# Block inversion on 16x16 instead of 32x32 blocks, a bias product over 128 rows, and a new order of all engines' lists

## The reference, cut to what matters

```python
def step(S, inp):                      # attention, token by token
    q_t, k_t, v_t, beta_t, alpha_t = inp
    S = S * alpha_t[..., None, None]
    kv = jnp.einsum('bhk,bhkv->bhv', k_t, S)
    S = S + jnp.einsum('bhk,bhv->bhkv', k_t, (v_t - kv) * beta_t[..., None])
    o_t = jnp.einsum('bhk,bhkv->bhv', q_t, S)
    return (S, o_t)
...
logits = flat_x @ W_router + b_router  # experts: the best 2 of 8
for e in range(NUM_EXPERTS):
    h = jax.nn.relu(flat_x @ W1[e] + b1[e])
    y = h @ W2[e] + b2[e]
    final_output = final_output + y * w[:, None]
```

## Time and profile before

| what | value |
|---|---|
| median of three runs | 1421.86 us |
| profiled execution: span | 1397.9 us |
| outside the span, runs less span | 21.2 to 25.0 us |
| PE, DVE busy in the span | 1199.9, 1164.4 us |
| ACT, POOL busy in the span | 832.0, 707.9 us |
| setup and first round | 0 to 133.8 us |
| 15 steady rounds | 133.8 to 1145.4 us, 67.44 us each |
| last round, routing's tail | 1145.4 to 1232 us |
| experts | 1232 to about 1371 us |

### The profile page before, as it was taken

How to read it: one execution, slowest core, us unless ns; L and a number is a source line. 1 busy time by engine, 2 the same in 40 slices (tenths; PEclk the granted TensorE clock), 3 DMA queues, 4 the chain that set the end, 5 groups by cost and what they waited for, 6 DMA issues and landing times.

```text
span 1397.9 us, 34191 instructions
## 1 busy us (share of the span) xinstructions
PE 1199.9 (86%) x12203; PEld 944.0 (68%) x12203; DVE 1164.4 (83%) x2531; ACT 832.0 (60%) x2536; POOL 707.9 (51%) x598
## 2 busy tenths in 40 slices
PE   0355999999999999999999999999999989479991
PEld 0233868686868687777777777777777767358881
DVE  6878898989898998989898989897989783578875
ACT  1252666666666666657566666756566655358884
POOL 3151727464555656473828292928192822235552
PEclk9997999999999999999999999999999998789996
DMA  6031212222221222131313141313121223432225
GB/s 208 0 98 32 73 35 73 47 69 62 54 63 53 62 54 64 52 68 48 84 34 91 28 98 25 103 28 88 30 85 43 73 55 98 104 96 78 76 65 181
DMA packets 163176, 97.10 MB, mean 69 GB/s; under 512 B 115623, under 2 KB 148269, under 8 KB 161988
## 3 DMA queue, kind: packets, MB, share of 16 engines
q1 hardware_dynamic: 124932, 82.25, 21.6%
q10 hardware_dynamic: 33536, 4.20, 2.1%
q0 software_dynamic: 4544, 8.47, 1.9%
HBM read 73.31 MB, written 24.61 MB: 70 GB/s over the span
## 4 chain that ended last, share of the span: by engine, by line
DVE 37%; PE 21%; POOL 17%; issue 10%; DMA 9%; SPq 3%; ACT 3%; POOLq 0%; DVEq 0%; ACTq 0%
DVE blkT L1060 9%; POOL kq L637 9%; DVE Y_sb L1056 9%; DMA blkN<-scr_n 4%; PE kx L1553 3%; POOL decay L629 3%; POOL rows_in L609 2%; DVE Gs L1204 2%; POOL kq L620 2%; DMA scr_n<-area 2%; PE rc L1717 2%; SPq L477 2%; DVE blkN L1047 1%; DVE area L1170 1%; DVE Y_sb L1043 1%
## 5 line engine op out<-in xcount | busy, mean ns | idle before, releaser
L637 POOL TENSOR_TENSOR kq<-tapA,area 128x256 f32<-128x256 f32 x256 | 252.0, 998 | 93.6 <-DVE area L1146 92.8
L758 ACT ACTIVATE area<-pj,taps 128x256 f32<-128x256 f32 x256 | 123.1, 481 | 142.7 <-PE pj L1567 136.5
L1056 DVE TENSOR_TENSOR Y_sb<-blkT,blkN 128x4 f32<-128x4 f32 (+18 forms) x304 | 169.5, 558 | 10.5
L609 POOL DMA_INDIRECT rows_in<-rowbuf,dest x64 | 64.6, 1009 | 202.1 <-DVE dest L1132 175.2
L1143 DVE SCALAR_TENSOR_TENSOR tapA<-pj,taps,tapA 128x256 f32<-128x256 f32 x256 | 122.2, 477 | 53.4 <-ACT tapA L758 51.6
L1553 PE MATMUL kx<-kq 128*128 128x128 f32 x1024 | 141.0, 285 | 20.0 <-ACT area L767 9.6
L1553 PEld LDWEIGHTS kx<-kq 128*128 128x128 f32 x1024 | 128.7, 197 | 38.4 <-issue 21.8
L620 POOL TENSOR_TENSOR kq<-kq,area 128x1024 f32<-128x1024 f32 x64 | 151.1, 2362 | 0.0
L1060 DVE TENSOR_REDUCE blkT<-Y_sb 128x2 f32<-128x4 f32 (+18 forms) x304 | 142.4, 469 | 5.2
L758 ACT ACTIVATE tapA<-pj,taps 128x256 f32<-128x256 f32 x256 | 123.0, 480 | 0.0
L1146 DVE SCALAR_TENSOR_TENSOR area<-pj,taps,area 128x256 f32<-128x256 f32 x256 | 121.4, 474 | 0.0
(11 more groups left out here) (307 smaller groups left out, 3613.2 us busy)
## 6 DMA issues: line engine op xcount, KB each, us to landing
area<-scr_alpha SPq DMA_DIRECT2D x32, 512.0 KB, 4.2
area<-scr_acum SPq DMA_DIRECT2D x32, 512.0 KB, 4.0
blkN<-scr_n SPq DMA_DIRECT2D x32, 256.0 KB, 4.4
area<-rows_in SPq DMA_DIRECT2D x39, 130.0 KB, 2.3
scr_n<-area SPq DMA_DIRECT2D x128, 32.0 KB, 1.6
area<-rows_out SPq DMA_DIRECT2D x4, 1024.0 KB, 8.1
rows_in<-rows_in SPq DMA_DIRECT2D x8, 260.0 KB, 3.8
kq<-in_x SPq DMA_DIRECT2D x4, 512.0 KB, 6.2
```

Of the source, the lines that this page charges most:

```text
L637: nc.gpsimd.tensor_tensor(dst[:, n % H, :], tapA[:, n % RING, :], tapB[:, n % RING, :], ALU.add).then_inc(conv_done, 1)
L758: ins = nc.scalar.activation(dst[:, n % RING, :], pj[n % 2][:, k:k + GT], ACT.Copy, scale=taps[:, t, k:k + 1])
L1056: ins = nc.vector.tensor_tensor(p4, bc(blkT[:, r0:, j:].rearrange("p r (o m) -> p r o m", o=1), [128, nr, w, wd]), bc(blkN[:, j:j + w, j:] ...
```

## The change

- **Blocks of 16.** The diagonal's 16x16 blocks, 128 of them, lie one in a partition. `bi` reads two quarters of every 32x32 block, rows of 64 bytes. `invert` has 8 pairs of product and sum (2, 18, 50, 98, 162, 242, 338 and 450 elements), three short operations of 128 and 16 elements, a memset, and a copy that writes the transpose, blkR. `rdiag` is gone.
- **From 16 to 32.** The inverses go out to scr_r and scr_a and come back into R's diagonal and TA. New steps: `y16` on PE (64 matmuls of 32x16, four 32-row bands in turn), `ye` on ACT (eviction of 128x256), `r16` on PE (64 of 16x16), `re` on DVE (four of 16x16x16), `td.0` and `td.1` on DVE (two transposes and one of 32x512).
- **New waits.** `nm` waits for the merge's y64_mm, `at` for o_mm, `kd` for sd_mm, `zt` for g_ready, `diag` for scale_ready, `ti` and `tj` for u_mm.
- **Bias.** b2_both has 128 rows, 126 of them zero, and L1713's matmul takes all 128.
- **Setup.** par_eye and its DMA go, scr_r is zeroed by one DMA.
- **Order.** ORDER is rewritten; the stand-ins stay 7 and 8.

```diff
-        SOLVE = [(j, 2) for j in range(BLK - 2, PAIR0 - 2, -2)] + [(j + i, 1) for j in range(PAIR0 - 2, -2, -2) for i in range(2)]
-        INV = 5 + 2 * len(SOLVE)
+        SOLVE = list(range(SUB - 2, -2, -2))
+        INV = 6 + 2 * len(SOLVE)
...
                         for side in range(2):
-                            sp.dma_start(blkN[64 * side:64 * side + 64, :, :], scr_n).then_inc(blk_in, 16)
+                            half_ = slice(SUB * side, SUB * side + SUB)
+                            sp.dma_start(blkN[64 * side:64 * side + 64, :, :], scr_n[:, half_, half_]).then_inc(blk_in, 16)
...
-                        sp.dma_start(scr_t.rearrange("q (a p) m -> p q a m", p=2)[0], blkT[0:64, :, :]).then_inc(t_out, 16)
+                        sp.dma_start(scr_r[:, 0:SUB, 0:SUB], blkR[0:64, :, :]).then_inc(t_out, 16)
+                        sp.dma_start(scr_a, blkT[0:64, :, :]).then_inc(t_out, 16)
...
+                        if g is not None:
+                            sp.wait_ge(u_mm, halves(g, GC - 1, U - 1))
+                        for b in range(NB):
+                            sp.dma_start(TA[BLK * b:BLK * b + SUB, :, :], a_blocks[b]).then_inc(t_in, 16)
...
+                elif s == INV - 1:
+                    ins = nc.vector.tensor_copy(blkR[:, :, :], blkT.rearrange("p r j -> p j r"))
                 else:
...
+                    j = SOLVE[(s - 5) // 2]
+                    n = SUB - 1 - j
+                    p4 = prod[:, 0:n * 2 * n].rearrange("p (r k m) -> p r k m", k=2, m=n)
...
                     elif step == "nm":
                         c, u = arg
                         dve.wait_ge(kk_ready, a * HALVES + U * c + u + 1)
+                        if g is not None:
+                            dve.wait_ge(y64_mm[c], rounds(g))
...
+            def small_blocks(g, a, r, step):
+
+                bank_free((step,), g, a, r)
+                n = GC * H * SUB
+                if step == "y16":
+                    pe.wait_ge(t_in, g * (32 * NB) + 32 * NB)
+                    y = ob[1][:, 0:n].rearrange("p (q j) -> p q j", j=SUB)
+                    for q in range(GC * H):
+                        for b in range(NB):
+                            r_ = slice(BLK * b, BLK * b + BLK)
+                            ins = mm(y[r_, q], Nm[r_, q // H, q % H, r_], TA[r_, q, :], start=True, stop=True)
...
-                    mm(o, ones[0:2, :], b2_both[:, ds(e, 1), :].rearrange("p o n -> p (o n)"), start=True, stop=False)
+                    mm(o, ones[:, :], b2_both[:, ds(e, 1), :].rearrange("p o n -> p (o n)"), start=True, stop=False)
```

Of the new ORDER the line that brings `st.0.1` behind the inversion's first steps:

```diff
+            first.13 taps.11 u.0.1 first.14 xl.1 taps.12 sd.0.0 inv.0 ue.0.1 last.6 kk.1.1 inv.1 proj.11 sm v.1.0
+            inv.2 taps.13 last.7 proj.12 st.0.1 taps.14 ktr.0.0 no.1 kd.0.0 inv.3 ks.1.0 last.8 sq.0.0 inv.4 proj.13
```

More of the change, by code:

```diff
@@ L264, in preln_delta_moe_kernel @@
-            st.1.1 xs.1 tj sc
+            proj.0 taps.0 first.0 last.0 y16 ye first.1 proj.1 al.0 taps.1 re r16 ka.0 taps.2 td.0 proj.2 taps.3
+            proj.3 first.2 v.0.0 me.1.0 first.3 aq.0 m.1.0 me.0.0 first.4 ac.0 ks.0.0 taps.4 first.5 proj.4 last.1
+            me.1.1 td.1 m.0.0 taps.5 m.1.1 scan.0 sp.0 taps.6 proj.5 first.6 v.0.1 me.0.1 al.1 first.7 proj.6 me.1.2
+            last.2 first.8 m.0.1 scale.0 proj.7 nm.0.0 rhs.0.0 m.1.2 diag.0 first.9 taps.7 ks.0.1 nm.0.1 no.0 m.0.2
+            me.0.2 scan.1 last.3 m.1.3 taps.8 st.0.0 proj.8 me.1.3 kk.0.0 nm.1.0 me.0.3 last.4 m.0.3 nm.1.1 rhs.0.1
@@ L303, in bank_of @@
                 return ("ob", "kx")[i], j % 2
+            if step in ("y16", "r16"):
+                return "ob", 1
             return None
@@ L317, in released @@
                 return ((x2_ready, chunks(b, i)),)
+            if step in ("y16", "r16"):
+                return (({"y16": y16_sb, "r16": r16_done}[step], rounds(b)),)
             if step == "m":
@@ L571, in _ @@
             nc.gpsimd.memset(T64[:, :, :, :], 0.0)
+            nc.gpsimd.memset(TA[:, :, :], 0.0)
             nc.gpsimd.memset(R, 0.0)
@@ L1245, in _ @@
             over_t = lambda t: bc(t.rearrange("p (t o) -> p t o", o=1), wide)
+            dve.wait_ge(sd_mm, NG * HALVES)
+            chain(nc.vector.memset(b2_both, 0.0), t_step, steps)
             dve.wait_ge(f_b2, 32)
             chain(nc.vector.tensor_scalar(b2_hi, b2_raw, WSCALE, None, ALU.mult), t_step, steps)
-            chain(nc.vector.scalar_tensor_tensor(out=b2_both, in0=b2_raw, scalar=WSCALE, in1=b2_hi, op0=ALU.mult,
+            chain(nc.vector.scalar_tensor_tensor(out=b2_both[0:2], in0=b2_raw, scalar=WSCALE, in1=b2_hi, op0=ALU.mult,
                                                  op1=ALU.subtract), t_step, steps)
@@ L1590, in finish @@
                 def finish(step, arg):
-                    if step == "m":
+                    if step in ("y16", "r16"):
+                        small_blocks(g, a, r, step)
+                    elif step == "m":
                         if arg != [1, 3]:
```

182 lines of the change are left out of this document (106 added, 76 removed).

## The result

The changed kernel takes **1534.07 us** (median of 4 runs, 1529.23 to 1535.36), the kernel before beside it 1422.34: ratio **1.078 [1.075, 1.080]**. Forecast were 1397.8, range 1364 to 1434. It is 7.8% slower, and it lies outside the range.

The account below looks back on a forecast made before the run. PE was taken to bound the steady rounds and experts, the inversion only the first round. First round -10, last round +2.4, steady rounds -4.5, experts -12: -24.1 us, 1421.9 to 1397.8 us, range 1364 to 1434.

Parts of the forecast that it names:

- The small products: y16 and r16 on PE: 1.2 us each, bounds 1.0 and 4.0, so PE's work rises 2.4 us a round.
- the forecast's 67.5: Steady round: 22.3 + 43.2 + 0.8 + 1.2 = 67.5 us against 67.8, -4.5 us over 15 rounds.
- POOL's lateness at `kk.0.1`: Head of the round: POOL's longer list puts kk.0.1 at 22.3 us instead of 20.2, 2.1 us later.
- No overlap of small products: Rival for y16 and r16: 4.0 us each instead of 1.2, +5.6 a round, 1470 us; chance 0.05.
- the grown wait: Rival at v.1.1: PE's wait for the scratch trip reaches 3.4 us, other pauses return, 1454 us; chance 0.15.
- I take 12: Experts: the 128-row bias product removes PE's 0.20 us gaps, 12 us gained, bounds 15.7 and 0.
- The 24 us outside the span being untouched: Whole run: 24 us outside the profiled span stays, so the -24.1 us holds for the runs' median.
- the reading that DVE is not the bound: Steady rounds: PE decides, not DVE; the rival that DVE was the bound gave 1220 us, chance 0.01.
- The first round: Inversion on the path here alone: 10 us of gain, bounds 6 and 13.
- The new wait at `v.1.1`: PE waits there for the update from rc1, behind blkN's landing: 1.2 us a round taken, 0.8 to 3.4 possible.
- DVE's 215: Inversion on DVE: 13.5 us less work a round, some 215 us in all.
- Last round and tail: Last round: only v stands beside the four new steps, so half of their 5 us shows, +2.4 us (0 to 5).

Follow-up runs that it names:

- (6): The four indirect DMAs moved behind last.11: changed kernel with bias on 2 rows 1.0499, also with quartered small products 1.0016, kernel before 1.0383.
- (8): Kernel before with a short POOL operation by the experts' indirect DMAs: ahead, 128-row bias 0.9916; ahead, 2-row 1.0003; between, 128-row 1.0002.
- (2): Bias product alone: kernel before with 128 rows, ratio 1.0025 and, on another chip, 1.0037; changed kernel with it back on 2 rows, 1.065.
- Experiment 1: The kernel before, unchanged, run for a second profile: 1418.0 us, span 1416.2.
- after: The changed kernel itself, against the kernel before: 1534.07 us, ratio 1.078.
- bias_undone: Changed kernel with the bias product back on 2 rows: 1514.6 us, ratio 1.065 to the kernel before.
- spread: Changed kernel with y16 in four pieces and r16 in two, projections and the long v product between: 1627.14 us, ratio 1.1465.
- y16_after_v: Changed kernel, bias on 2 rows, y16 behind the first v product, v.0.1 and ks.0.0 ahead of the first merge: 1563.75 us, ratio 1.1021.
- quarter: Changed kernel, bias on 2 rows, y16 and r16 of 16 matmuls each with four times the columns (values not the reference's): 1475.1 us, ratio 1.0392.
- before_again: The kernel before, unchanged, profiled a second time: 1418.0 us.
- sc_later_quarter: Changed kernel, bias on 2 rows, indirect DMAs behind last.11, y16 and r16 of 16 four-times-wider matmuls (values not the reference's): 1396.33 us, ratio 1.0016.

## Why the prediction was wrong

**The step that failed: "The small products ... I take 1.2 each, with bounds 1.0 and 4.0".** The rate was right and the bounds were of the wrong thing. I bounded the time of a pass, and the cost was in getting passes to the engine. Two things held them back: the indirect DMAs beside `y16`, and the end of a block of 256 instructions, mostly in `r16` (6). Measured in the round shown: `y16` 5.3, `r16` 2.9, so 8.2 instead of 2.4; +5.8 (over the 15 rounds from the second on 5.1 and 2.5 in the mean, +5.2). The clock falls on top: 572.68 to 580.00 at 0.74 is 7.32 x 0.26 = 1.9 us, and the projection at 569.06, at twice its pitch, 0.3. 67.5 + 5.8 + 2.2 = 75.5, and this round took 75.5 (563.83 to 639.37); the mean of 74.64 has rounds without a halt in `r16` in it. That the rest comes out at the forecast's 67.5 is in part luck: POOL's lateness at `kk.0.1`, 2.1 us in the sum, did not show. I had the four DMAs in the earlier trace rows, and read them only as POOL's time. What neighbours they would have on PE I never asked.

**"No overlap of small products"** gave 1470 and a head longer by 5.6 us a round, which is near what came. But its reason was wrong. The Trainium skill, "TensorE: Matmul & The Clock Gate", section "Back-to-back issue gap", puts starts at least about 25 ns apart; here 128 passes in four bands took 1.26 us, 10 ns each, and the measurement decides. The right size from a false mechanism is no confirmation. (The forecast's 1454 for the grown wait is 1448 by its own numbers: 70.9 less 67.8, the base of its other sums, is 3.1 and not 3.5.)

**"I take 12" for the experts:** -3.2 or so without pauses (8), and in the executions with pauses a loss (2), since PE's gap had kept the pairs of indirect DMAs apart more often.
**"The 24 us outside the span being untouched":** wrong. Experiment 1 shows 2 us outside the span; the experts took 151.6 us there and 131.4 in the execution profiled, which had no such pauses.

**Right:** the reading that DVE is not the bound (-180 us of DVE's work bought nothing in the rounds). The first round: -9 to -12 us of -10. The new wait at `v.1.1`: 13.7 / 15 = 0.9 us a round of 1.2. Its reason was even stronger than said: blkN comes in two DMAs a round, of 256 KB each before and 64 KB each after, so a quarter of the bytes and not half, and they land after 3.4 us instead of 4.4. `kk` waits 5.3 us in all for 1024 products, so POOL's lateness is no matter: PE is later. DVE's 215 came to 180; part of the lack is that the scan L1187 went from 2.9 to 3.2 us, and the rest is below. Last round and tail: +8 where 2.4 were put; there `r16` alone takes 4.8 us, with a halt of 3.4 at a block's end.

**Still open.** Which part of the instruction supply POOL's indirect DMAs hold up: no row shows it, the theory rests on times that agree (after, bias_undone, spread, y16_after_v, quarter, before_again) and on one move (6). Why the next block comes late (how far ahead PE asks for it) and how much the halts at a block's end cost by themselves: the account of them rests on times that agree in all 82, and on their being gone with a quarter of the instructions. How much of the 7.2 us is pauses and how much the clock: no run parted them. Why some chips or executions have the experts' pauses and others not. Whether the change pays with a cheap place for the indirect DMAs: sc_later_quarter says that its ceiling is no change from before (1.0016), not a gain.

## What to carry to other kernels

Before a burst of very short instructions is put on one engine, look at what the other engines issue at that time: the price of an instruction alone in a quiet place (10 ns here) is no price beside POOL's indirect DMAs, and 256 instructions in 1.26 us are gone before the next 256 are there. Fewer and longer instructions help where the work allows them: 32 passes of 64 columns took 0.65 us and had no halt. Where "issue" pauses appear on two or three engines at once, look at POOL's timeline for DMA_INDIRECT rows 0.30 us apart, and put POOL work between them. And ask of a profiled execution, before its sum is carried to the median, whether its span and its runs differ by a constant or by a stage.

## What the runs showed that I had not expected

- 128 passes of 32x32 by 16 columns in four bands take 1.26 us.
- Four indirect DMAs in a row slow PE to one to five passes per 0.74 us until some 0.8 to 0.9 us after the last has ended: 566.94 and 567.87 (after), 599.54 and 600.30 (spread), 584.76 and 585.65 (y16_after_v).
- Without any of them, PE halts in such bursts for up to 4 us (mostly 1 to 2) where a block of 256 instructions ends, until 1.2 to 1.6 us after the packet with the next has landed (82 halts, eight runs).
- DVE's product of 50 columns took 1.5 us in the mean, longer than that of 450:

```profile
L1089 DVE TENSOR_TENSOR prod<-blkT,blkN 128x50 f32<-128x50 f32 x16 | 24.0, 1499 | 0.5
...
L1089 DVE TENSOR_TENSOR prod<-blkT,blkN 128x450 f32<-128x450 f32 x16 | 10.1, 629 | 0.6
```

In the round looked at it ran from 611.44 to 613.02, and POOL's L670 from 611.06 to 612.96: it ended when POOL's was done. The scan at 586.07 took 4.04 us beside POOL's L650 (586.07 to 587.97), and 2.50 at 597.06. That such operations of the two hold each other up was not tried by itself.
